# Folding the squares for the norm of an attention block, with the order of the step rewritten on three engines

## The chip, the cores and the metric

The kernel runs on one core of one Trainium2 chip. The metric is the device time of one execution in microseconds (us). The engines are named as in the profile: PE is TensorE (matmul), PEld its weight loads, DVE is VectorE, ACT is ScalarE, POOL is GpSimd, SP is SyncE, which issues most of the DMAs.

## What is computed

One block of a network with a gated, decaying linear attention in chunks of 128 positions, followed by a gated feed-forward layer. For a batch of 4 sequences of 256 positions, width 512, 32 heads of 128 in 8 groups that share keys and values:

```python
q = rope(h @ Wq.T); k = rope(h @ Wk.T); v = h @ Wv.T      # h: layernorm of x, modulated
decay = where(causal, exp(G_i - G_j), 0)                    # G: running sum of the decay rates in a chunk
y_intra = (q_i . k_j * decay) @ (v * dt)                    # inside a chunk
y_inter = (q * exp(G)) @ state                              # from the chunk before
y = y_intra + y_inter
rms = sqrt(mean(square(y), axis=-1) + 1e-5)                 # over the 128 of a head
y = y / rms * gnorm_w
y = y * (gate * sigmoid(gate))                              # gate = h @ Wg.T
x = x + ga * (y @ Wo.T)
x = x + gb * ffn(modulated layernorm of x)
```

The change lies in how `mean(square(y))` is summed over the 128 numbers of a head, and in the order in which the attention's work is issued.

## The kernel before

The attention loops over 8 groups of 4 heads (`groups`): seven passes of a hardware loop, and the last group written out. In a group there are 8 steps, `step(g, t)`, one for each tile of 128 positions; t // 2 is the sequence b, and c = t % 2 the chunk in it. "Even step" below is c = 0, "odd step" c = 1. The last four tiles of the last group have no projections left to do and are written as `tail`. The feed-forward layer follows and isn't touched.

The work on a tile is spread over two steps. Step t projects q and gate for four tiles ahead (`q_block`, `g_block`: 12 matmuls each, since every f32 product is made of three products of a rounded high part and a low part, lines L54 to L56), does the scores of tile t (`scores`, into ps_s) and its output (`y_product`, into ps_y), and multiplies the finished tile t - 1 by Wo (`out_product`, which needs z_hi and z_lo of tile t - 1). An even step also does the scores of the next chunk with this chunk's keys (`cross_scores`) and the keys and values of the next sequence (`kv_batch`, 24 matmuls of 256 columns); an odd step has a second product in `y_product` and transposes the keys (`k_turn`).

Each engine has its own queue and works through it in the order in which the code is written; there is no scheduler. Semaphores tie the queues together. The chain that turns ps_y into z runs over all of them: ACT squares ps_y, once in f32 into `work` and once rounded into `sq_hi`; DVE subtracts the two (`sq_lo`) and multiplies ps_y by the gate (into z); PE sums both parts over the 128 partitions with two matmuls by a matrix of ones (`square_sum`, L686 and L688, into ps_ss); ACT takes the logarithm (L854) and the exponential (L857) of it, `inverse_rms`; DVE multiplies z by that (`normed_z`); ACT rounds z to `z_hi` (L861), and DVE makes `z_lo`. Beside it ACT makes the gate's sigmoid in three passes, `exp_gate` (L755), and after DVE's `cap` (L980) a logarithm (L760) and an exponential (L762), `sigmoid`. `probabilities` (L1160) multiplies the scores by the decay on DVE. The squares, the probabilities and z share one buffer, `work`. POOL does one product of the rotation of each step (`rotate_q_sin`, L1299) and in even steps the causal mask of the next sequence (`mask`, L1292), which waits for `exp_g` on ACT (L770). Weights of the next group are split by DVE into high and low parts: one head in each of t = 1 to 4, keys and values at t = 5, and Wo at t = 0.

Of the kernel before, what the change touches and what calls it, by code (L numbers as in the profile page):

```python
# [10 lines left out]
P = 128  # L11
# [183 lines left out]
def block_attention(nc, cst, x1, hT_hi, hT_lo, tok, modT, gnorm, ident, modrow, gT_dram,  # L195
                    x_in, cT_in, wmod_in, wq_in, wg_in, wkv_in, wo_in, win_in, rows_in,
                    gnorm_in, cst_in, wgu_in, norm_rows, raw_pair):
    with ExitStack() as ctx:
        def sb(name, shape, dt=F32):
            return ctx.enter_context(nc.sbuf_tensor(name, shape, dt))  # L200
# [10 lines left out]
        wkv_hi, wkv_lo = (sb(n, [P, KT, 2 * D], F32R) for n in ("wkv_hi", "wkv_lo"))  # L211
        wo_hi, wo_lo = (sb(n, [P, GRP, HID], F32R) for n in ("wo_hi", "wo_lo"))
# [26 lines left out]
        prob_tail = sig[:].rearrange("p (h i) -> p h i", h=GRP)  # L239
# [10 lines left out]
        win, win_hi, win_lo = (w[:].rearrange("p (k h) -> p k h", k=KT) for w in (q_cos, sq_hi, sq_lo))  # L250
# [6 lines left out]
        zT = gT = [sq[0:H], rms[0:H]]  # L257
# [71 lines left out]
        sq_done = sem("sq_done")  # L329
        sqhi_done = sem("sqhi_done")  # L330
# [179 lines left out]
        def _(pe):  # L510
# [152 lines left out]
            def y_product(g, t, tail=False):  # L663
# [8 lines left out]
                weights = prob_tail if tail else prob[:]  # L672
                nc.tensor.matmul(ps_y[:], v[:, b % 2, c], weights.rearrange("p h i -> p (h i)"),  # L673
# [9 lines left out]
            def square_sum(g, t):  # L683

                pe.wait_ge(sqhi_done, g * 8 + (t + 1))
                nc.tensor.matmul(ps_ss[:], ones[:], sq_hi[:], start=True, stop=False)  # L686
                pe.wait_ge(sqlo_done, g * 8 + (t + 1))
                nc.tensor.matmul(ps_ss[:], ones[:], sq_lo[:], start=False, stop=True)\  # L688
                    .then_inc(ss_ready, 1)

            def step(g, t, project, next_batch, next_group):
# [4 lines left out]
                if project:  # L696
                    q_block(g, t)
                out_product(g, t)
                if c == 1 and next_batch:
                    k_turn(g, b)  # L700
                y_product(g, t)
                if project:
                    g_block(g, t, 0, KT - 1)
                square_sum(g, t)
                if project:
                    g_block(g, t, KT - 1, KT)
                if c == 0 and next_batch:
                    kv_batch(g, b)

            def tail(g, t):  # L710
# [5 lines left out]
                y_product(g, t, True)  # L716
# [27 lines left out]
        def _(act):  # L744
# [43 lines left out]

            def copy_kT(g, b):
# [54 lines left out]
            def squares(g, t, tail=False):  # L844
                if tail:
# [843 lines left out]
```

## Time and profile before

| | |
|---|---|
| median of 3 runs | 1111.58 us (1111.44 to 1113.81) |
| the profiled execution | 1113.59 us, its span 1111.8 us |
| PE busy | 1067.2 us, 96% |
| DVE busy | 767.0 us, 69% |
| ACT busy | 550.8 us, 50% |
| POOL busy | 206.1 us, 19% |
| mean granted clock of PE | 0.984 |

The span is the time from the first to the last instruction of the profiled execution. Busy times are sums of the durations of instructions; those of PE overlap, since a matmul starts before the one before it has ended, so starts tell more of PE than durations do. The granted clock is a share of 2.4 GHz.

### The profile page before, as it was taken

The page shows a single profiled execution, that of the slowest core. Times are in us where ns is not written, and L with a number is a line of the kernel's source. Part 1 is how long each engine was busy: PE and PEld are TensorE (multiplying, and loading weights), DVE is VectorE, ACT ScalarE, POOL GpSimd, SP SyncE. Part 2 cuts the span into 40 slices and gives each one's busy share as a digit, 9 for nine tenths or more (in the row PEclk, how much of TensorE's full clock was granted, in tenths as well). Part 3 has the DMA queues.
Part 4 walks back from the last instruction along what each step waited for, and adds up shares of the span by engine and source line. Part 5 has one row for each costly group of instructions (what it writes and reads, how often), then busy time and mean ns, then how long its engine had stood idle before and what let it go on. Part 6 is the DMA issues. An engine that isn't in the chain of part 4 may idle for free. (4 is left out here: it accounts for less than half of the span.)

```text
span 1111.8 us, 14213 instructions
## 1 busy us (share of the span) xinstructions
PE 1067.2 (96%) x4680; PEld 808.9 (73%) x4680; DVE 767.0 (69%) x1492; ACT 550.8 (50%) x1133; POOL 206.1 (19%) x131
## 2 busy tenths in 40 slices
PE   4879999999999999999999999999999969999898
PEld 1757777777777777777777777777776449888786
DVE  5777786877787678868876887778676686434411
ACT  3445556665555666555666555566655434222300
POOL 3412211212221121122111222211121530000000
PEclk9989999999999999999999999999999979999999
DMA  6121301220131013112201320131031622111011
GB/s 223 58 69 49 124 30 38 75 75 19 38 113 38 19 38 113 38 28 83 96 19 38 97 54 19 38 113 38 19 95 24 204 99 72 49 45 57 29 38 38
DMA packets 37464, 70.89 MB, mean 64 GB/s; under 512 B 2936, under 2 KB 19576, under 8 KB 35520
## 3 DMA queue, kind: packets, MB, share of 16 engines
q1 hardware_dynamic: 36720, 70.16, 19.9%
q10 hardware_dynamic: 720, 0.43, 0.1%
q8 instruction: 13, 0.21, 0.1%
q14 instruction: 11, 0.09, 0.0%
HBM read 68.33 MB, written 2.24 MB: 63 GB/s over the span
## 5 line engine op out<-in xcount | busy, mean ns | idle before, releaser
L1299 POOL TENSOR_TENSOR q_sin<-q_sin,cst 128x512 f32<-128x512 f32 x64 | 82.8, 1293 | 390.9 <-ACT q_sin L751 390.9
L1292 POOL TENSOR_TENSOR dec<-dec,future 128x1024 f32<-128x1024 f32 x31 | 80.3, 2590 | 273.6 <-ACT expg L770 273.6
L848 ACT ACTIVATE work<-ps_y 128x512 f32<-128x512 f32 x64 | 38.4, 599 | 186.4 <-PE ps_y L673 185.6
L54 PE MATMUL ps_gt<-hT_hi,wg_hi 128*128 128x512 f32 x256 | 125.7, 491 | 3.7 <-DVE sg L986 3.7
L54 PE MATMUL ps_q<-hT_hi,wq_hi 128*128 128x512 f32 x256 | 125.5, 490 | 2.8 <-DVE q_cos L966 2.3
L54 PE MATMUL ps_o<-wo_hi,z_hi 128*128 128x512 f32 x260 | 104.1, 400 | 2.4 <-DVE z_lo L49 2.4
L55 PE MATMUL ps_o<-wo_lo,z_hi 128*128 128x512 f32 x260 | 103.4, 398 | 0.0
L56 PE MATMUL ps_o<-wo_hi,z_lo 128*128 128x512 f32 x260 | 103.0, 396 | 0.0
L56 PE MATMUL ps_q<-hT_hi,wq_lo 128*128 128x512 f32 x256 | 101.2, 395 | 0.0
L55 PE MATMUL ps_gt<-hT_lo,wg_hi 128*128 128x512 f32 x256 | 100.7, 393 | 0.0
L56 PE MATMUL ps_gt<-hT_hi,wg_lo 128*128 128x512 f32 x256 | 100.7, 393 | 0.0
L55 PE MATMUL ps_q<-hT_lo,wq_hi 128*128 128x512 f32 x256 | 100.4, 392 | 0.0
L750 ACT ACTIVATE q_sin<-ps_q 64x512 f32<-64x512 f32 x64 | 38.1, 596 | 111.0 <-PE ps_q L56 110.9
L49 DVE TENSOR_TENSOR sq_lo<-work,sq_hi 128x512 fp32r<-128x512 f32 x64 | 44.6, 697 | 62.1 <-ACT sq_hi L849 62.1
L780 ACT ACTIVATE dec<-dec,scal 128x128 f32<-128x128 f32 x256 | 81.7, 403 | 1.4 <-DVE scal L944 1.4
L1160 DVE SCALAR_TENSOR_TENSOR work<-ps_s,scal,dec 128x128 f32<-128x128 f32 x240 | 67.6, 345 | 20.5 <-DVE z_lo L49 11.0
L1190 DVE TENSOR_TENSOR work<-work,rms 128x512 f32<-128x512 f32 x64 | 44.3, 692 | 52.4 <-ACT rms L857 52.4
L54 PE MATMUL ps_kv<-wkv_hi,hT_hi 128*128 128x256 f32 x256 | 73.6, 288 | 0.0
L55 PE MATMUL ps_kv<-wkv_lo,hT_hi 128*128 128x256 f32 x256 | 73.2, 286 | 0.0
L56 PE MATMUL ps_kv<-wkv_hi,hT_lo 128*128 128x256 f32 x256 | 73.1, 286 | 0.0
L966 DVE TENSOR_TENSOR q_cos<-ps_q,cst 128x512 f32<-128x512 f32 x64 | 44.1, 690 | 41.7 <-ACT q_sin L751 41.6
L54 PEld LDWEIGHTS ps_gt<-hT_hi,wg_hi 128*128 128x128 f32 x256 | 48.5, 189 | 27.0 <-issue 14.4
(239 smaller groups left out, 2553.0 us busy)
## 6 DMA issues: line engine op xcount, KB each, us to landing
dec<-gT_dram SPq DMA_DIRECT2D x32, 512.0 KB, 5.4
raw_q<-wq_in SPq DMA_DIRECT2D x32, 256.0 KB, 2.7
raw_g<-wg_in SPq DMA_DIRECT2D x32, 256.0 KB, 2.9
raw_o<-wo_in SPq DMA_DIRECT2D x8, 1024.0 KB, 7.3
raw_pair<-wkv_in SPq DMA_DIRECT2D x8, 512.0 KB, 4.7
raw_pair<-wgu_in SPq DMA_DIRECT2D x6, 512.0 KB, 3.3
raw_gu<-wgu_in SPq DMA_DIRECT2D x5, 512.0 KB, 3.4
qT<-wmod_in SPq DMA_DIRECT2D x2, 1024.0 KB, 7.0
```

Of the source, the lines that this page charges most:

```text
L49: return engine.tensor_tensor(lo, full, hi.bitcast(F32), ALU.subtract)
L54: pe.matmul(out, w_hi, x_hi, start=first, stop=False)
L55: pe.matmul(out, w_hi, x_lo, start=False, stop=False)
L56: return pe.matmul(out, w_lo, x_hi, start=False, stop=last)
L750: nc.scalar.activation(q_sin[0:64], ps_q[64:128, :], ACT.Copy)
L780: last = nc.scalar.activation(cell, cell, ACT.Exp, bias=scal[:, bn * CPB + c, 0, h:h + 1])
L848: nc.scalar.activation(sq, ps_y[:], ACT.Square).then_inc(sq_done, 1)
L966: nc.vector.tensor_tensor(q_cos[:].rearrange("p (b i) -> p b i", b=2), ps_q[:].rearrange("p (b i) -> p b i", b=2), cosT, ALU.mult)\
L1160: last = nc.vector.scalar_tensor_tensor(dest[:, h], ps_s[:, h * P:(h + 1) * P], scal[:, t, 1, h:h + 1], dec[:, b % 2, h, c], ALU.mult, ALU ...
L1190: nc.vector.tensor_tensor(z[:], z[:], rms[:].rearrange("p (h i) -> p h i", h=GRP), ALU.mult).then_inc(z_done, 1)
L1292: nc.gpsimd.tensor_tensor(cells, cells, future[:].unsqueeze(1).broadcast_to([P, GRP * CPB, CHUNK]), ALU.add).then_inc(mask_done, 1)
L1299: nc.gpsimd.tensor_tensor(q2, q2, sinT, ALU.mult).then_inc(qsin_done, 1)
```

## The change

The square of ps_y is now taken once, in two halves of 64 partitions (`sq_low`, `sq_top`); DVE adds the halves (`sum_squares`); ACT rounds the sum into the lower half of one tile, `sq_parts`, and DVE puts the low part into its upper half. One matmul by ones then sums high and low part together. `work` is replaced by three buffers of their own, and `win_lo` gets one of its own. The high parts of the weights are cast by ACT and no longer by DVE. And the order of the step is another on PE, ACT and DVE:

```diff
-        work = sb("work", [P, GRP, CHUNK])
-        prob, z = work, work
-        sq = work[:].rearrange("p h i -> p (h i)")
-        sq_hi, sq_lo = sb("sq_hi", [P, HALF], F32R), sb("sq_lo", [P, HALF], F32R)
+        prob, z = sb("prob", [P, GRP, CHUNK]), sb("z", [P, GRP, CHUNK])
+        sq_parts = sb("sq_parts", [P, HALF], F32R)
+        sq_top, sq_low = sb("sq_top", [P // 2, HALF]), sb("sq_low", [P // 2, HALF])
+        sq_sum = sb("sq_sum", [P // 2, HALF])
+        win_lo = sb("win_lo", [P, KT, P], F32R)
         rms = sb("rms", [P, HALF])
...
             def square_sum(g, t):
                 pe.wait_ge(sqhi_done, g * 8 + (t + 1))
-                nc.tensor.matmul(ps_ss[:], ones[:], sq_hi[:], start=True, stop=False)
                 pe.wait_ge(sqlo_done, g * 8 + (t + 1))
-                nc.tensor.matmul(ps_ss[:], ones[:], sq_lo[:], start=False, stop=True)\
+                nc.tensor.matmul(ps_ss[:], ones[:], sq_parts[:], start=True, stop=True)\
                     .then_inc(ss_ready, 1)
             def step(g, t, project, next_batch, next_group):
                     cross_scores(g, t)
                 if project:
                     q_block(g, t)
+                y_product(g, t)
                 out_product(g, t)
+                if project:
+                    g_block(g, t, 0, 2)
                 if c == 1 and next_batch:
                     k_turn(g, b)
-                y_product(g, t)
                 if project:
-                    g_block(g, t, 0, KT - 1)
-                square_sum(g, t)
-                if project:
-                    g_block(g, t, KT - 1, KT)
+                    g_block(g, t, 2, KT)
                 if c == 0 and next_batch:
                     kv_batch(g, b)
+                square_sum(g, t)
...
+            def round_squares(g, t):
+                act.wait_ge(sqsum_done, g * 8 + (t + 1))
+                nc.scalar.activation(sq_parts[0:64], sq_sum[:], ACT.Copy).then_inc(sqhi_done, 1)
...
-            def squares(g, t, tail=False):
-                if tail:
-                    act.wait_ge(zlo_done, g * 8 + (t + 1))
+            def squares(g, t):
                 act.wait_ge(y_ready, g * 8 + (t + 1))
-                nc.scalar.activation(sq, ps_y[:], ACT.Square).then_inc(sq_done, 1)
-                nc.scalar.activation(sq_hi[:], ps_y[:], ACT.Square).then_inc(sqhi_done, 1)
+                nc.scalar.activation(sq_low[:], ps_y[0:64], ACT.Square)
+                nc.scalar.activation(sq_top[:], ps_y[64:128], ACT.Square).then_inc(sq_done, 1)
+            def split_head_hi(g, j):
+                act.wait_ge(wh_loaded, g * 128 + 32 * (j + 1))
+                nc.scalar.activation(wq_hi[:, j], raw_q[:], ACT.Copy)
+                nc.scalar.activation(wg_hi[:, j], raw_g[:], ACT.Copy).then_inc(wh_hi_done, 1)
+            def split_kv_hi(g):
+                act.wait_ge(kv_loaded, g * 16 + 16)
+                nc.scalar.activation(wkv_hi[:], raw_kv[:], ACT.Copy).then_inc(kv_hi_done, 1)
+            def split_o_hi(g):
+                act.wait_ge(o_ready, g * 8 + 1)
+                act.wait_ge(wo_loaded, g * 16 + 16)
+                nc.scalar.activation(wo_hi[:], raw_o[:], ACT.Copy).then_inc(wo_hi_done, 1)
...
                 b, c = t // 2, t % 2
                 swap(g, t)
                 squares(g, t)
+                if next_group and 1 <= t <= GRP:
+                    split_head_hi(g + 1, t - 1)
+                if next_group and t == GRP + 1:
+                    split_kv_hi(g + 1)
+                round_squares(g, t)
                 if c == 1:
                     copy_kT(g, b)
                 decays(g, t + 1)
-                inverse_rms(g, t)
+                if t == 0:
+                    split_o_hi(g)
                 exp_gate(g, t)
-                split_z_hi(g, t)
-                sigmoid(g, t)
                 if c == 0:
+                    sigmoid(g, t)
+                    inverse_rms(g, t)
                     copy_v(g, b)
+                    split_z_hi(g, t)
                     exp_g(g, b)
+                else:
+                    inverse_rms(g, t)
+                    sigmoid(g, t)
+                    split_z_hi(g, t)
...
-            def probabilities(g, t, tail=False):
-                b, c = t // 2, t % 2
-                dest = prob_tail if tail else prob
-                if tail and t == 4:
-                    dve.wait_ge(sg_done, g * 8 + 8)
-                if not tail:
-                    dve.wait_ge(zlo_done, g * 8 + (t + 1))
+            def probabilities(g, t):
+                tile = t % NT
                 dve.wait_ge(s_ready, g * 8 + (t + 1))
                 dve.wait_ge(dec_done, g * 8 + (t + 1))
                 for h in range(GRP):
                     last = nc.vector.scalar_tensor_tensor(
-                        dest[:, h], ps_s[:, h * P:(h + 1) * P], scal[:, t, 1, h:h + 1],
-                        dec[:, b % 2, h, c], ALU.mult, ALU.mult)
+                        prob[:, h], ps_s[:, h * P:(h + 1) * P], scal[:, tile, 1, h:h + 1],
+                        dec[:, tile // 2 % 2, h, tile % 2], ALU.mult, ALU.mult)
                 last.then_inc(prob_done, 1)
+            def sum_squares(g, t):
+                dve.wait_ge(sq_done, g * 8 + (t + 1))
+                nc.vector.tensor_tensor(sq_sum[:], sq_low[:], sq_top[:], ALU.add).then_inc(sqsum_done, 1)
             def gated_y(g, t):
                 half = t // 4
-                dve.wait_ge(sqhi_done, g * 8 + (t + 1))
-                split_lo(nc.vector, sq_lo[:], sq, sq_hi[:]).then_inc(sqlo_done, 1)
-                dve.wait_ge(sqlo_done, g * 8 + (t + 1))
+                dve.wait_ge(zlo_done, g * 8 + (t + 1))
                 dve.wait_ge(sg_done, g * 8 + (4 * half + 4))
                 nc.vector.tensor_tensor(z[:], ps_y[:].rearrange("p (h i) -> p h i", h=GRP),
                                         sg[:, half, :, rows_of(t)], ALU.mult).then_inc(zz_done, 1)
+                dve.wait_ge(sqhi_done, g * 8 + (t + 1))
+                split_lo(nc.vector, sq_parts[64:128], sq_sum[:], sq_parts[0:64]).then_inc(sqlo_done, 1)
...
                 heads, keys = next_group and 1 <= t <= GRP, next_group and t == GRP + 1
-                probabilities(g, t)
+                gate(g, t - 1)
                 if c == 1:
                     rotate_k(g, b, t)
-                gate(g, t - 1)
                 rotate_q_cos(g, t)
                 if c == 0:
                     cross_probabilities(g, t)
-                if heads:
-                    split_head_hi(g + 1, t - 1)
-                if keys:
-                    split_kv_hi(g + 1)
+                sum_squares(g, t)
                 rotate_q_add(g, t)
+                gated_y(g, t)
                 add_out(g, t)
-                gated_y(g, t)
                 if heads:
                     split_head_lo_g(g + 1, t - 1)
+                    split_head_lo_q(g + 1, t - 1)
                 if keys:
                     split_kv_lo(g + 1)
                 if c == 0:
                     copy_scalars(g, b)
                 if t == 0:
-                    split_o_hi(g)
+                    split_o_lo(g)
+                probabilities(g, t + 1)
+                cap(g, t)
                 normed_z(g, t)
-                cap(g, t)
-                if heads:
-                    split_head_lo_q(g + 1, t - 1)
                 split_z_lo(g, t)
-                if t == 0:
-                    split_o_lo(g)
...
```

`tail` follows in the same manner: DVE's `sum_squares` stands ahead of `gated_y`, ACT's `round_squares` behind `squares`, `squares` no longer waits for z_lo, and the probabilities go to `prob` and not to the buffer of the sigmoid. Ahead of the loop DVE does the probabilities of tile 0.

ACT, an even step from the decays of the next tile to the rounding of expg (the names in brackets are the semaphores that a row waits for). Before:

```order
L780 ACTIVATE dec<-dec,scal 128x128 x4
L854 ACTIVATE rms<-ps_ss,eps_col 128x512 [waits ss_ready]
L857 ACTIVATE rms<-rms 128x512 [waits lnss_done]
L755 ACTIVATE sig<-ps_gt 128x512 [waits g_ready]
L861 ACTIVATE z_hi<-work 128x512 [waits z_done]
L760 ACTIVATE sig<-sig 128x512 [waits cap_done]
L762 ACTIVATE sig<-sig 128x512 [waits lsig_done]
L785 REGISTER_ALU
L787 ACTIVATE v<-ps_kv 128x256 [waits kv_ready]
L767 REGISTER_ALU
L770 ACTIVATE expg<-dec 128x512 [waits cross_done,dec_loaded]
```

The same stretch of an even step of the changed kernel:

```order
L790 ACTIVATE sq_parts<-sq_sum 64x512 [waits sqsum_done]
L779 ACTIVATE dec<-dec,scal 128x128 x4
L754 ACTIVATE sig<-ps_gt 128x512 [waits g_ready]
L759 ACTIVATE sig<-sig 128x512 [waits cap_done]
L761 ACTIVATE sig<-sig 128x512 [waits lsig_done]
L855 ACTIVATE rms<-ps_ss,eps_col 128x512 [waits ss_ready]
L858 ACTIVATE rms<-rms 128x512 [waits lnss_done]
L784 REGISTER_ALU
L786 ACTIVATE v<-ps_kv 128x256 [waits kv_ready]
L878 ACTIVATE z_hi<-z 128x512 [waits z_done]
L766 REGISTER_ALU
L769 ACTIVATE expg<-dec 128x512 [waits cross_done,dec_loaded]
```

The two passes of the sigmoid now stand ahead of the two of the inverse norm and of the rounding of z, where they stood behind all three.

DVE, from the end of an even step that splits a head (t = 4) into the odd one that follows. Before:

```order
L1190 TENSOR_TENSOR work<-work,rms 128x512 [waits rms_done,zz_done]
L980 TENSOR_SCALAR sig<-sig 128x512 [waits esig_done]
L49 TENSOR_TENSOR wq_lo<-raw_q,wq_hi 128x512
L49 TENSOR_TENSOR z_lo<-work,z_hi 128x512 [waits zhi_done]
L1160 SCALAR_TENSOR_TENSOR work<-ps_s,scal,dec 128x128 [waits dec_done,s_ready,zlo_done]
L1160 SCALAR_TENSOR_TENSOR work<-ps_s,scal,dec 128x128 x3
L950 REGISTER_ALU
L953 TENSOR_TENSOR q_cos<-ps_kv,cst 128x256 [waits rope_done,v_done]
L954 TENSOR_TENSOR q_cos<-ps_kv,cst 128x2x64
L956 TENSOR_TENSOR q_cos<-ps_kv,cst 128x2x64
L959 TENSOR_TENSOR kr<-q_cos 128x256 [waits kparts_done]
L986 SCALAR_TENSOR_TENSOR sg<-ps_gt,gnorm,sig 128x512 [waits sig_done]
```

The same place of the changed kernel:

```order
L1179 SCALAR_TENSOR_TENSOR prob<-ps_s,scal,dec 128x128 [waits dec_done,s_ready]
L1179 SCALAR_TENSOR_TENSOR prob<-ps_s,scal,dec 128x128 x3
L1004 TENSOR_SCALAR sig<-sig 128x512 [waits esig_done]
L1214 TENSOR_TENSOR z<-z,rms 128x512 [waits rms_done,zz_done]
L49 TENSOR_TENSOR z_lo<-z,z_hi 128x512 [waits zhi_done]
L1010 SCALAR_TENSOR_TENSOR sg<-ps_gt,gnorm,sig 128x512 [waits sig_done]
L974 REGISTER_ALU
L977 TENSOR_TENSOR q_cos<-ps_kv,cst 128x256 [waits rope_done,v_done]
L978 TENSOR_TENSOR q_cos<-ps_kv,cst 128x2x64
L980 TENSOR_TENSOR q_cos<-ps_kv,cst 128x2x64
L983 TENSOR_TENSOR kr<-q_cos 128x256 [waits kparts_done]
L989 REGISTER_ALU [waits kr_done]
```

The probabilities of the next tile, which wait for that tile's scores (s_ready), stood behind `cap`, `normed_z` and `z_lo`; now all three stand behind them.

## Rows read from the trace of the kernel before

**Rows 1.** The page: the span, and each engine's busy time, share and instructions.

```profile
span 1111.8 us, 14213 instructions
PE 1067.2 (96%) x4680; PEld 808.9 (73%) x4680; DVE 767.0 (69%) x1492; ACT 550.8 (50%) x1133; POOL 206.1 (19%) x131
```

**Rows 2.** Busy time by stretches: from:to, length, each engine's busy time, clock, DMA.

```profile
100.00:860.00 760.00, 760.00 (x3346) 574.87 (x3345) 578.32 (x1168) 445.60 (x916) 150.43 (x88) 1.00 0.19 56
```

**Rows 3.** Groups of instructions, 100 to 860: count | busy, mean ns | idle before.

```profile
L688 PE MATMUL ps_ss<-sq_lo,ones_r 128*128 128x512 f32 x59 | 23.3, 396 | 0.0
L750 ACT ACTIVATE q_sin<-ps_q 64x512 f32<-64x512 f32 x58 | 34.6, 596 | 103.9 <-PE ps_q L56 103.9
```

**Rows 4.** Timeline of PE, an even step and an odd one: start, us, instruction.

```profile
415.64 1.02 PE L659 MATMUL ps_s<-qT,kT 128*128 128x512 f32 x2
...
426.08 0.40 PE L688 MATMUL ps_ss<-sq_lo,ones_r 128*128 128x512 f32 x1
426.31 0.39 PE L54 MATMUL ps_gt<-hT_hi,wg_hi 128*128 128x512 f32 x1
...
429.87 1.02 PE L659 MATMUL ps_s<-qT,kT 128*128 128x512 f32 x2
...
433.48 0.40 PE L54 MATMUL ps_o<-wo_hi,z_hi 128*128 128x512 f32 x1
...
436.49 1.02 PE L668 MATMUL ps_y<-cross,v 128*128 128x512 f32 x2
437.36 1.02 PE L673 MATMUL ps_y<-work,v 128*128 128x512 f32 x2
...
441.45 1.02 PE L659 MATMUL ps_s<-qT,kT 128*128 128x512 f32 x2
```

**Rows 5.** Timeline of ACT over the same boundary between steps.

```profile
426.51 0.69 ACT L854 ACTIVATE rms<-ps_ss,eps_col 128x512 f32<-128x512 f32 x1 [0.29 <-PE ps_ss L688]
427.23 0.63 ACT L857 ACTIVATE rms<-rms 128x512 f32<-128x512 f32 x1
...
428.70 0.64 ACT L861 ACTIVATE z_hi<-work 128x512 fp32r<-128x512 f32 x1 [0.34 <-DVE work L1190]
429.23 0.62 ACT L760 ACTIVATE sig<-sig 128x512 f32<-128x512 f32 x1
429.88 0.63 ACT L762 ACTIVATE sig<-sig 128x512 f32<-128x512 f32 x1
430.42 0.36 ACT L787 ACTIVATE v<-ps_kv 128x256 f32<-128x256 f32 x1
```

**Rows 6.** Timeline of DVE over the same boundary.

```profile
427.97 0.69 DVE L1190 TENSOR_TENSOR work<-work,rms 128x512 f32<-128x512 f32 x1 [0.77 <-ACT rms L857]
428.58 0.42 DVE L980 TENSOR_SCALAR sig<-sig 128x512 f32<-128x512 f32 x1
...
429.51 0.69 DVE L49 TENSOR_TENSOR z_lo<-work,z_hi 128x512 fp32r<-128x512 f32 x1
430.99 1.13 DVE L1160 SCALAR_TENSOR_TENSOR work<-ps_s,scal,dec 128x128 f32<-128x128 f32 x4 [0.78 <-DVE z_lo L49]
...
432.88 1.18 DVE L959 TENSOR_TENSOR kr<-q_cos 128x256 f32<-128x256 f32 x1
...
435.52 1.01 DVE L44 CAST wq_hi<-raw_q 128x512 fp32r<-128x512 f32 x1
436.46 0.41 DVE L44 CAST wg_hi<-raw_g 128x512 fp32r<-128x512 f32 x1
```

**Rows 7.** Timeline of POOL in the odd step.

```profile
431.38 2.40 POOL L1292 TENSOR_TENSOR dec<-dec,future 128x1024 f32<-128x1024 f32 x1 [8.49 <-ACT expg L770]
434.96 1.29 POOL L1299 TENSOR_TENSOR q_sin<-q_sin,cst 128x512 f32<-128x512 f32 x1 [1.18 <-ACT q_sin L751]
```

**Rows 8.** Timeline of PE, two of its waits; the last is the tail's.

```profile
56.02 0.47 PE L54 MATMUL ps_q<-hT_hi,wq_hi 128*128 128x512 f32 x1 [2.27 <-DVE q_cos L966]
...
901.69 0.47 PE L54 MATMUL ps_o<-wo_hi,z_hi 128*128 128x512 f32 x1 [2.40 <-DVE z_lo L49]
```

**Rows 9.** PE by stretches behind those waits: length, busy, granted clock, DMA.

```profile
56.00:60.00 4.00, 2.96 (x12) 1.00 0.00 0
902.00:906.00 4.00, 4.00 (x12) 0.57 0.02 4
```

More of the change, by code:

```diff
@@ L210, in block_attention @@
         wg_hi, wg_lo = (sb(n, [P, GRP, KT, D], F32R) for n in ("wg_hi", "wg_lo"))
-        wkv_hi, wkv_lo = (sb(n, [P, KT, 2 * D], F32R) for n in ("wkv_hi", "wkv_lo"))
-        wo_hi, wo_lo = (sb(n, [P, GRP, HID], F32R) for n in ("wo_hi", "wo_lo"))
+        wo_hi, wo_lo = (sb(n, [P, GRP, HID], F32R, "right") for n in ("wo_hi", "wo_lo"))
+        wkv_hi, wkv_lo = (sb(n, [P, KT, 2 * D], F32R, "right") for n in ("wkv_hi", "wkv_lo"))
         raw_q, raw_g = sb("raw_q", [P, KT, D]), sb("raw_g", [P, KT, D])
@@ L249, in block_attention @@
         silu_c = sb("silu_c", [P, KT * B])
-        win, win_hi, win_lo = (w[:].rearrange("p (k h) -> p k h", k=KT) for w in (q_cos, sq_hi, sq_lo))
+        win, win_hi = (w[:].rearrange("p (k h) -> p k h", k=KT) for w in (q_cos, sq_parts))
         rows = cross[:, 1, 0:2 * H].rearrange("p (r h) -> p r h", r=2)
@@ L329, in block_attention @@
         sq_done = sem("sq_done")
+        sqsum_done = sem("sqsum_done")
         sqhi_done = sem("sqhi_done")
@@ L661, in scores, with y_product @@
                                  start=True, stop=True).then_inc(s_ready, 1)
-            def y_product(g, t, tail=False):
+            def y_product(g, t):
                 b, c = t // 2, t % 2
@@ L671, in y_product @@
                 pe.wait_ge(prob_done, g * 8 + (t + 1))
-                weights = prob_tail if tail else prob[:]
-                nc.tensor.matmul(ps_y[:], v[:, b % 2, c], weights.rearrange("p h i -> p (h i)"),
+                nc.tensor.matmul(ps_y[:], v[:, b % 2, c], prob[:].rearrange("p h i -> p (h i)"),
                                  start=c == 0, stop=True).then_inc(y_ready, 1)
@@ L715, in tail @@
                     out_product(g, t)
-                y_product(g, t, True)
+                y_product(g, t)
                 if c == 0:
@@ L881, in tail @@
                     decays(g, t + 1)
-                squares(g, t, True)
+                squares(g, t)
+                round_squares(g, t)
                 if t == 5:
@@ L1108, in _ @@
                     dve.wait_ge(win_split, 1)
-                    split_lo(nc.vector, win_lo, win, win_hi).then_inc(win_split, 1)
+                    split_lo(nc.vector, win_lo[:], win, win_hi).then_inc(win_split, 1)
             dve.wait_ge(tables_loaded, 16)
@@ L1234, in tail @@
                     gate(g, t - 1)
-                    probabilities(g, t, True)
                     add_out(g, t)
                     guard_gate(0)
+                sum_squares(g, t)
                 gated_y(g, t)
@@ L1243, in tail @@
                 if t < NT - 1 and t != 5:
-                    probabilities(g, t + 1, True)
+                    probabilities(g, t + 1)
                 if t == 4:
@@ L1254, in tail @@
                 if t == 5:
-                    probabilities(g, t + 1, True)
+                    probabilities(g, t + 1)
                 if t == 6:
@@ L1271, in stats_of @@
                 norm2.vector_stats(dve, tile)
+            probabilities(0, 0)
             groups(dve, step, tail)
```

10 lines of the change are left out of this document (3 added, 7 removed).

## The prediction

> **What bounds the kernel now.** I read the page first: PE is busy 96% of the span, DVE 69%, ACT 50% [rows 1]. A share is an average, so the next view is the stretch that holds the attention's loop, 100 to 860 us: PE is busy in all 760 of 760 us, DVE in 578, ACT in 446 [rows 2]. Busy times of PE overlap, so I checked starts on the timeline: matmuls of 512 columns start 0.23 us apart without a hole [rows 4], and the group of the second sum of squares has no idle time before it, 59 times out of 59 [rows 3]. In the loop nothing but the number of matmuls counts. Two steps take 441.45 - 415.64 = 25.81 us [rows 4].
>
> The other engines run in PE's shadow, and how much shadow there is can be read at the boundary from an even step to an odd one. The odd step's scores start at 429.87, the product by Wo at 433.48, 3.61 us later [rows 4]. It needs z_lo, which ends at 429.51 + 0.69 = 430.20 [rows 6], so 3.3 us early. The chain behind that is logarithm 426.51, exponential 427.23, z times it 427.97, z_hi 428.70, z_lo 429.51 [rows 5, 6]. It ends early because the sum of squares is done some 3.8 us ahead of the scores (426.08 against 429.87), and because ACT does the sigmoid's two passes behind z_hi [rows 5].
>
> **What goes.** One of the two matmuls by ones in each of the 64 tiles: 0.23 us from start to start [rows 4] (its busy 0.396 us [rows 3] is overlap). 0.46 us for a pair of steps, 14.7 us in all. This is the whole gain, as the loop has no other idle time of PE to win.
>
> **What moves, odd step.** The sum of squares now stands last in the step, the product of y ahead of the one by Wo, and on DVE the next tile's probabilities, which need the next scores, ahead of cap, z and z_lo. So z's chain can't end until the next step's scores have been done, and in even steps ACT puts the whole sigmoid ahead of the inverse norm. I lay the old durations along the new order, with 0 at the start of the odd step's scores. DVE starts the probabilities 430.99 - 429.87 = 1.12 after them and needs 1.13 [rows 4, 6]. DVE starts an independent instruction 0.08 before the last one ends (427.97 + 0.69 against 428.58), so cap runs from 2.17 to 2.59 [rows 6]. An engine takes up another's result 0.04 later (428.66 to 428.70): the sigmoid's logarithm starts at 2.63, its exponential 0.65 later at 3.28, the next independent pass 0.54 after that at 3.82, by the starts 429.23, 429.88, 430.42 [rows 5]. That pass is the logarithm of the squares; exponential 0.72 later at 4.54, until 5.17; z from 5.28 to 5.97 (0.11 and 0.69, as 427.86 to 427.97); z_hi from 6.01 to 6.65; z_lo from 6.69 to 7.38; PE can go on at 7.42 [rows 5, 6]. PE itself is there at 3.61, plus the two products of y that now come first, 0.87 each (436.49 to 437.36): 5.35 [rows 4]. **The product by Wo waits 2.07 us in every odd step.**
>
> **Even step.** There inverse_rms comes first, and only cap ties the chain to the scores: cap ends at 2.59, the sigmoid's passes start at 2.63 and 3.28, z_hi at 3.82, z_lo ends at 5.19, PE could go on at 5.23, and it arrives at 3.61 + 0.87 + 0.87 = 5.35 (cross scores and y) [rows 4 to 6]. It fits by 0.12 us. Where a head or the keys were split, DVE comes to the probabilities about 0.3 late, and PE waits 0.1 to 0.2. Over all pairs I take 0.1.
>
> **The sum of squares in odd steps.** z_lo is late, so are the mask, the keys and the squares behind it. ACT makes expg 0.54 after z_hi's start, at 6.55; it takes what the sigmoid's passes take, 0.62, and POOL's mask then runs 2.40, from 7.21 to 9.61 [rows 5, 7]. DVE comes to kr at about 8.8. Kr took 1.18 us and ended at 434.06, 0.28 after the mask's end at 433.78; the cast of wq_hi took 1.01 and ended at 436.53, 0.28 after POOL's product ended at 436.25, while the same cast beside an idle POOL took 0.41 [rows 6, 7]. So such a DVE instruction is held until POOL is through: kr ends at 9.9. POOL follows at once with its product (1.29, to about 11.0), and the new sum of the two halves, started at 10.4, is held until then and ends at 11.5. Rounding 11.6 to 12.2, and behind q's sum and the gated product the low part from 12.7 to 13.4. PE gets there at 7.42 + 24 x 0.23 + 0.22 for the transposes = 13.16. It waits 0.3 us more.
>
> The Trainium skill, "SBUF — State Buffer", section "Who interferes with whom", has the rule: a VectorE instruction with two SBUF inputs and a GpSimd instruction exclude each other, the later one blocked for the whole of the other. The two rows agree. With the rule the pair loses this 0.3 us, 9 us in all; if the new sum, on 64 partitions only, were not held, it would lose nothing here, and the total below would be 9 us lower.
>
> **Added work.** The squares are two passes on 64 partitions, where the nearest row is 0.596 us for 64x512 [rows 3], so they cost what the two old ones did. Rounding is one more such pass, the sum one more DVE instruction of 0.69; both are in the chain above. The weights' high parts on ACT: two casts a step, about 0.64 each, as z_hi [rows 5], keys and Wo two and four times that at most. They stand between the squares, done at about 9.0, and the rounding, which in odd steps waits for DVE until 11.5: hidden. If that cover were gone, they would cost at most 1.3 us in four steps of eight. The weights' loads wait for the low parts, which come earlier now, and those of the decays for the probabilities, also earlier: nothing on SP. The start of the loop costs nothing.
>
> **The tail.** Four tiles whose chain is exposed at the end (PE waits 2.40 for z_lo at 901.69 [rows 8]). Sum and rounding lengthen each tile's chain by 0.73 + 0.68, one square pass and one matmul go. Where other work of PE covers it, nothing is lost, and at all four 5 us. I take 2.
>
> **Sum.** The step runs 60 times, 30 pairs: -0.46 + 2.07 + 0.3 + 0.1 = +2.0 us, 60 us; with the tail 62. On the profiled span that is 1111.8 + 62 = 1174; this execution took 1113.59 us against a median of 1111.58 of the runs, so its span is as good a base as the median: 1174 us, 5.6% slower. (Of no change a measurement can tell about 0.2%.)
>
> **Rivals.**
> - The clock falls. PE sat still 2.40 us before 901.69, and in 902 to 906 the granted clock is 0.57, near the lower level of 1.2 GHz; after 2.27 us before 56.02 it stayed at 1.00 in 56 to 60 [rows 8, 9]. My 2.07 is below both, and PE is fully busy around it, which speaks against. If it fell each time as at 902, where (1 - 0.57) x 4 = 1.7 us of PE's work is lost, that would be 30 x 1.7 = 51 more, 1225; if at some, 1190 and up. 10%.
> - A shorter chain. If links are 0.1 faster in the new order, or the new sum isn't held by POOL, the odd step loses 1.3 to 2.0 instead of 2.4: 1140 to 1158. 9%.
> - More waits than I see (SP's loads, the keys, an even step that fits by 0.12 only): 0.5 us a pair and more, 1190 to 1205. 7%.
> - No slower at all: PE finds z_lo ready in the odd step. That needs the chain to end 5.31 us after the scores, not 7.38. It could if the inverse norm's 1.35 us ran while ACT waits for cap, which the queue's order forbids as a queue runs in its own order everywhere in this trace; then z would start at cap's end as in an even step, and only the saving would be left: 1111.6 - 13.8 + 2 = 1100. The deciding point is whether the logarithm of the squares starts before the scores are done. 4%.
>
> **How the numbers follow.** The forecast, 1158 to 1190, has 70%. For 8 in 10 I take in the upper part of the shorter chain and the lower part of more waits and the clock: 1152 to 1200. Slower 0.95, within 0.2% 0.01, faster 0.04, the last being the fourth rival's.
>
> **What the changed profile would show.** PE's idle before the first ps_o matmul (L54), released by z_lo, about 30 times and 50 to 65 us in all; the logarithm of ps_ss in even steps behind the sigmoid's exponential and 3.8 us after the scores' start; an idle before ps_ss of about 0.3 in odd steps, with the sum of squares longer than 0.69 beside POOL; pairs of 27.8 us instead of 25.8. A granted clock below 1.00 between 100 and 860 us would show the first rival; a z_lo that ends before the product of y the fourth.

## The result, and the profile after

The changed kernel takes 1202.51 us (median of 4 runs, 1199.5 to 1204.31) against 1112.69 of the kernel before beside it: ratio 1.079, 95% interval 1.076 to 1.081, 7.9% slower. The forecast, 1174 (range 1158 to 1190, 1152 to 1200 for eight in ten), had the sign and the place, and missed the size. The page of the changed kernel (span; busy time, share and instructions of each engine) answers to [rows 1]:

```profile
span 1201.6 us, 14252 instructions
PE 1089.0 (91%) x4616; PEld 805.2 (67%) x4616; DVE 775.1 (65%) x1485; ACT 651.5 (54%) x1268; POOL 205.2 (17%) x131
```

PE has 64 matmuls fewer and is busy only 91% of a longer span. The waits of the changed kernel from 100 to 930 us (engine, line and what it waited for: us in total, times, longest) say where it stands still:

```profile
PE ps_o L54 <- DVE z_lo L49: 56.7, 29, 2.0
PE ps_o L54 <- ACT z_hi L878: 1.9, 1, 1.9
PE ps_ss L687 <- DVE sq_parts L49: 1.8, 10, 0.2
```

So once in every odd step, 30 times, the product by Wo waits for z. How that comes about is on the timeline (start, duration, instruction, and in brackets the idle time before it) of one odd step and the start of the next, PE first:

```profile
439.11 1.02 PE L660 MATMUL ps_s<-qT,kT 128*128 128x512 f32 x2
...
443.57 1.02 PE L673 MATMUL ps_y<-prob,v 128*128 128x512 f32 x2
446.62 0.49 PE L54 MATMUL ps_o<-wo_hi,z_hi 128*128 128x512 f32 x1 [2.03 <-DVE z_lo L49]
446.95 0.39 PE L55 MATMUL ps_o<-wo_lo,z_hi 128*128 128x512 f32 x1
447.18 0.39 PE L56 MATMUL ps_o<-wo_hi,z_lo 128*128 128x512 f32 x1
...
452.27 0.40 PE L56 MATMUL ps_gt<-hT_hi,wg_lo 128*128 128x512 f32 x1
452.70 0.47 PE L687 MATMUL ps_ss<-sq_parts,ones_r 128*128 128x512 f32 x1
453.01 1.02 PE L660 MATMUL ps_s<-qT,kT 128*128 128x512 f32 x2
```

The same stretch on ACT and DVE:

```profile
441.66 0.63 ACT L759 ACTIVATE sig<-sig 128x512 f32<-128x512 f32 x1 [4.02 <-DVE sig L1004]
442.32 0.63 ACT L761 ACTIVATE sig<-sig 128x512 f32<-128x512 f32 x1
442.86 0.67 ACT L855 ACTIVATE rms<-ps_ss,eps_col 128x512 f32<-128x512 f32 x1
443.56 0.63 ACT L858 ACTIVATE rms<-rms 128x512 f32<-128x512 f32 x1
...
445.02 0.63 ACT L878 ACTIVATE z_hi<-z 128x512 fp32r<-128x512 f32 x1 [0.56 <-DVE z L1214]
```

```profile
440.17 1.13 DVE L1179 SCALAR_TENSOR_TENSOR prob<-ps_s,scal,dec 128x128 f32<-128x128 f32 x4 [0.83 <-PE ps_s L660]
441.21 0.42 DVE L1004 TENSOR_SCALAR sig<-sig 128x512 f32<-128x512 f32 x1
444.30 0.69 DVE L1214 TENSOR_TENSOR z<-z,rms 128x512 f32<-128x512 f32 x1 [2.67 <-ACT rms L858]
445.68 0.69 DVE L49 TENSOR_TENSOR z_lo<-z,z_hi 128x512 fp32r<-128x512 f32 x1 [0.69 <-ACT z_hi L878]
```

Read it as a chain from the scores: probabilities 1.06 after them, cap at 2.10, the sigmoid at 2.55, the logarithm of the squares only at 3.75, z_lo done at 7.26 (446.37). ACT sat still for 4.02 us before the sigmoid; in the last 2.4 of them, from 439.27 on, the squares' sum (the ps_ss matmul started at 438.88, for 0.39) lay ready. The forecast had 1.12, 2.17, 2.63, 3.82 and 7.38.

The second view is the granted clock (from:to, length, busy times, clock, DMA), over the loop and in the 3 us behind two such waits, after 1.93 us at 132.79 and after 1.93 us at 160.94:

```profile
100.00:930.00 830.00, 767.65 (x3256) 564.10 (x3255) 576.70 (x1147) 536.42 (x1035) 149.46 (x88) 0.98 0.17 51
132.99:135.99 3.00, 3.00 (x14) 2.44 (x14) 2.84 (x7) 2.89 (x6) 3.00 (x2) 1.00 0.00 0
161.14:164.14 3.00, 3.00 (x11) 2.36 (x11) 2.84 (x7) 2.79 (x5) 3.00 (x2) 0.71 0.00 0
```

In the second stretch 11 matmuls start instead of 14: for a part of it the clock was at its lower level, 1.2 GHz. This follows 11 of the 30 waits. An odd step without it takes 13.9 us (about 14.2 at t = 7), one with it 15.03 to 15.17.

The span cut at the loop's first scores and at the tail's:

| | before | changed | changed, second trace |
|---|---|---|---|
| start | 78.43 | 82.23 | 78.70 |
| loop, 60 steps | 775.96 | 854.87 | 854.57 |
| tail and feed-forward | 257.41 | 264.50 | 264.93 |
| span | 1111.8 | 1201.6 | 1198.2 |

### The profile page after: what moved, and what is told of

Read it like the earlier page. It is cut to its first block and busy times, and to the rows that moved or that the text cites. A ratio compares the mean times of both kernels' runs of the same rounds, so it can differ in the third digit from the quotient of the medians.

```text
span 1201.6 us, 14252 instructions
## 1 busy us (share of the span) xinstructions
PE 1089.0 (91%) x4616; PEld 805.2 (67%) x4616; DVE 775.1 (65%) x1485; ACT 651.5 (54%) x1268; POOL 205.2 (17%) x131
## 5 line engine op out<-in xcount | busy, mean ns | idle before, releaser
L54 PE MATMUL ps_o<-wo_hi,z_hi 128*128 128x512 f32 x260 | 115.3, 444 | 62.3 <-DVE z_lo L49 59.8
L759 ACT ACTIVATE sig<-sig 128x512 f32<-128x512 f32 x64 | 40.4, 632 | 182.2 <-DVE sig L1004 182.2
L1179 DVE SCALAR_TENSOR_TENSOR prob<-ps_s,scal,dec 128x128 f32<-128x128 f32 x256 | 72.0, 344 | 102.4 <-PE ps_s L660 102.4
L54 PEld LDWEIGHTS ps_o<-wo_hi,z_hi 128*128 128x128 f32 x260 | 52.3, 201 | 117.3 <-ACT z_hi L878 75.4
L56 PE MATMUL ps_o<-wo_hi,z_lo 128*128 128x512 f32 x260 | 110.5, 425 | 0.0
L54 PE MATMUL ps_gt<-hT_hi,wg_hi 128*128 128x512 f32 x256 | 105.2, 411 | 3.7 <-DVE sg L1010 3.7
L1214 DVE TENSOR_TENSOR z<-z,rms 128x512 f32<-128x512 f32 x64 | 44.1, 689 | 82.2 <-ACT rms L858 82.2
L49 DVE TENSOR_TENSOR z_lo<-z,z_hi 128x512 fp32r<-128x512 f32 x64 | 45.6, 712 | 60.3 <-ACT z_hi L878 60.3
L790 ACT ACTIVATE sq_parts<-sq_sum 64x512 fp32r<-64x512 f32 x64 | 40.5, 632 | 66.7 <-DVE sq_sum L1198 65.5
L660 PE MATMUL ps_s<-qT,kT 128*128 128x512 f32 x128 | 65.8, 596 | 3.8 <-DVE qT L998 3.2
```

The costliest lines, as they stand in the source:

```text
L49: return engine.tensor_tensor(lo, full, hi.bitcast(F32), ALU.subtract)
L54: pe.matmul(out, w_hi, x_hi, start=first, stop=False)
L56: return pe.matmul(out, w_lo, x_hi, start=False, stop=last)
L660: nc.tensor.matmul(ps_s[:].rearrange("p (h i) -> p h i", h=GRP), kT[:, b % 2, c * P:(c + 1) * P], qT[:, half, :, rows_of(t)], start=True, ...
L759: nc.scalar.activation(sig[:], sig[:], ACT.Ln, bias=1.0).then_inc(lsig_done, 1)
L790: nc.scalar.activation(sq_parts[0:64], sq_sum[:], ACT.Copy).then_inc(sqhi_done, 1)
```

## The experiments

The before runs beside the kernels have medians of 1113.2 to 1114.37 us. Fences below leave out what the text doesn't need.

**1 to 3: undo one move, the other, both.** ACT's (with c == 0):

```diff
                 if c == 0:
-                    sigmoid(g, t)
                     inverse_rms(g, t)
+                    sigmoid(g, t)
                     copy_v(g, b)
```

DVE's:

```diff
-                probabilities(g, t + 1)
                 cap(g, t)
+                probabilities(g, t + 1)
                 normed_z(g, t)
```

> Edit: in even steps ACT does the inverse norm ahead of the sigmoid again (as odd steps do); all else as in the changed kernel. Theory (the order on ACT makes z_lo late): the odd step's wait for z_lo before the product by Wo, 1.95 us in each of 30 odd steps, goes; z_lo then ends 5.2 us after the scores' start, PE comes at 5.35. With it the half-clock stretches behind these waits go (11 of them, 12.7 us of the loop). Left: waits before the sum of squares, 0.3 to 0.5 in odd steps. Time 1118 to 1132 us. Rival (the added work on ACT and DVE - casts, sum, rounding - is what PE waits for): z_lo stays late by a us or more, 1160 us or more.

> Edit: DVE does cap ahead of the next tile's probabilities; ACT's order as changed (sigmoid ahead of the inverse norm in even steps). Theory (cap waits for the next scores only because it is queued behind the probabilities): the sigmoid is then done before the next scores, the inverse norm starts on time, and nothing before the product by Wo waits. Time 1104 to 1114, about the kernel before or a little under it. Rival (ACT's order alone is the fault, as z waits for the inverse norm behind two more passes): the wait in odd steps shrinks to between 0.5 and 1.5 us, 1125 to 1160.

> Edit: both of these together. Theory: PE waits nowhere in the loop; only the saved matmul counts, 0.46 us a pair, 14 us, against some 7 us that the tail lost: 1103 to 1110, pairs of steps of 25.35 us. Rival (the added DVE and ACT work of the folded squares costs more than it saves): the sum of squares in odd steps waits 0.3 us or more, 1112 or more.

Measured: ACT's move undone 1133.16 us (ratio 1.0185, 1.0162 to 1.0209), DVE's undone 1109.64 (0.9964, 0.9953 to 0.9976), both undone 1102.71 (0.990, 0.9881 to 0.9918). The second lies in its interval; the first is 1.2 us above its own (1118 to 1132), the third 0.3 below (1103 to 1110). Odd steps take mostly 11.98, 11.33 and 11.33 us (12.3 in the first kernel at t = 7, 12.05 in the second at t = 1), even steps 14.21, 13.94 and 13.94: where DVE's move stays, even steps are 0.27 longer too. With both undone PE is without a hole again, as in [rows 2]; the window of the loop in that kernel:

```profile
100.00:830.00 730.00, 730.00 (x3241) 555.65 (x3240) 571.12 (x1138) 524.86 (x1024) 146.35 (x87) 1.00 0.19 58
```

and on ACT the logarithm doesn't wait for the sigmoid:

```profile
422.84 0.69 ACT L855 ACTIVATE rms<-ps_ss,eps_col 128x512 f32<-128x512 f32 x1 [2.50 <-PE ps_ss L687]
423.56 0.64 ACT L858 ACTIVATE rms<-rms 128x512 f32<-128x512 f32 x1
424.10 0.61 ACT L759 ACTIVATE sig<-sig 128x512 f32<-128x512 f32 x1
```

What follows: the long wait before the product by Wo is the work of the two moves together. Against both undone, ACT's order alone costs 7 us, DVE's alone 30, both 100 us: either engine's order alone still leaves a way on which the squares' norm doesn't go through the next scores; together they close it. With DVE's move alone z still stands behind the probabilities, and z_lo ends 5.36 us after the scores, 0.03 too late for PE: its start behind that and a wait before the sum of squares make the odd step 0.65 longer.

**4 and 5: fill the wait.** Into the changed kernel, between v's product and Wo's in odd steps, 8 matmuls whose result nobody reads (1.84 us), or 3 (0.69 us):

```diff
                 y_product(g, t)
+                if c == 1:
+                    for _ in range(8):      # 3 in the other kernel
+                        nc.tensor.matmul(ps_x[:], ones[:], hT_hi[:, 0, 0:HALF], start=True, stop=True)
                 out_product(g, t)
```

> Edit: the changed kernel, with 8 matmuls of 512 columns by ones into ps_x, which nobody reads then, put into the gap of the odd step between the product of y and the product by Wo (8 x 0.23 = 1.84 us in a gap of about 2.1). No wait is taken away. Theory (the idle gap makes the granted clock fall in about one odd step of three, which costs 12.7 us of the loop): no stretch at half clock in the loop, odd steps all 13.7 to 13.9 us, 1187 to 1192 us. Rival (the clock falls for another reason, or the long steps have another cause): still 15.06 us in a third of the odd steps, and 1202 us or more.

> The changed kernel with three products whose result nobody reads between v's product and Wo's in the odd steps (0.69 us of the about 2 us that TensorE waits there). Eight of them kept the clock at 1.00 through the loop and took 11 us off the span. Theory (the clock falls because of the length of the uninterrupted idle stretch, which is 1.3 us now): no half-clock stretch in the loop, every odd step 13.9 us, 1190 to 1193 us as with eight. Rival (it is the amount of work in the step, which three products change little): odd steps of 15.0 us remain, 4 to 11 of them, 1195 to 1202 us.

Measured: 1191.55 us (1.071, 1.0684 to 1.0737) and 1192.33 (1.071, 1.0687 to 1.0734), some 10 us under the changed kernel with more work for PE. The waits and the clock with three:

```profile
PE ps_o L54 <- DVE z_lo L49: 36.6, 29, 1.3
```

```profile
100.00:920.00 820.00, 776.65 (x3345) 568.93 (x3344) 576.12 (x1150) 535.62 (x1033) 150.71 (x88) 1.00 0.17 52
```

The 30 waits are 1.20 to 1.34 us long, and the clock is at 1.00 throughout; both times lie in their intervals; all odd steps but t = 7 take 13.9 us, those about 14.2. The loop takes 844.54 us instead of 854.57 to 854.87: the clock's part of the loss is 10.2 us. (An odd step with the half clock loses 1.15 us, but the even step behind it is 0.3 shorter, 13.95 against 14.24, presumably since the other engines have caught up.) So the falls come from the idle time before the product by Wo. Whether the length of the one wait decides, as I expected, or the idle time of the whole step, is not shown: three products shorten both at once, and no run parts them.

**6 and 7: a longer wait, and the changed kernel again.** One more pass on ACT in even steps, behind the sigmoid; nobody reads what it writes:

```diff
                     sigmoid(g, t)
+                    nc.scalar.activation(sq_low[:], sq_top[:], ACT.Copy)
                     inverse_rms(g, t)
```

> The changed kernel with one more pass of ScalarE on 64 partitions, whose result nobody reads, between the sigmoid and the logarithm of the squares in the even steps. TensorE's wait for z_lo in the odd steps is then longer by about 0.53 us, 2.5 instead of 1.9 to 2.0. In the changed kernel 11 of the 30 waits of 1.89 to 2.03 us were followed by a stretch at half clock; of the waits of 2.27 to 2.61 us at the start and the end of ten traces 16 of 19 were. Theory (how often the clock falls goes with the length of the wait): 20 or more of the 30 waits are followed by a stretch at half clock, so 30 x 0.53 = 16 us for the wait and 9 to 19 more stretches of 1.15 us, 10 to 22 us: 1225 to 1242 us. Rival (which waits it falls after is set by something else, such as the place in the program): again about 11, so 16 us more than the changed kernel, 1216 to 1221.

> The changed kernel once more, for a second trace of it. Theory (the fall of the clock after a wait of 1.9 to 2.0 us is a matter of chance): another set of 6 to 16 odd steps has the stretch at half clock, the other odd steps take 13.9 us, and the start of the loop, 3.8 us late in the first trace, is at 78 to 82 us. Rival (it belongs to certain steps): the same 11 steps. The time is 1198 to 1205 us by either.

Measured: 1221.66 us (1.0984, 1.0947 to 1.1021) and 1200.54 (1.0789, 1.0755 to 1.0822). The waits are now 2.40 to 2.57 us, and 17 of 30 are followed by a lower clock, two of them here:

```profile
130.34:133.34 3.00, 3.00 (x14) 2.42 (x14) 2.84 (x7) 2.89 (x6) 3.00 (x2) 1.00 0.00 0
159.05:162.05 3.00, 3.00 (x9) 2.32 (x9) 2.84 (x7) 2.80 (x5) 3.00 (x2) 0.58 0.00 0
```

More than 11, fewer than the 20 I expected; 30 x 0.51 = 15.3 us of wait and six more such stretches make up the loop's 21 us (875.69 against 854.7). The time, 1221.66, lies between the two intervals, 1216 to 1221 and 1225 to 1242. The theory holds in direction, my size of it doesn't. The second trace of the changed kernel has again 11 falls of 30, but in other steps: only four waits of the thirty are hit in both. They are spread evenly, behind every second to fourth wait and never behind two in a row; with the longer waits two in a row occur three times. What picks them stays open. The time, 1200.54, lies in the interval that both shared, 1198 to 1205. The start is at 78.70, so the 3.8 us at the start of the first trace weren't the change's.

**8: the tail without the fold.** On top of both moves undone, the last four tiles alone square 128 partitions twice and sum with two matmuls:

```diff
+                nc.scalar.activation(sig[:], ps_y[:], ACT.Square)
+                nc.scalar.activation(sq_parts[:], ps_y[:], ACT.Square).then_inc(sqhi_done, 1)
...
+                pe.wait_ge(sqhi_done, g * 8 + (t + 1))
+                nc.tensor.matmul(ps_ss[:], ones[:], sq_parts[:], start=True, stop=False)
+                pe.wait_ge(sqlo_done, g * 8 + (t + 1))
+                nc.tensor.matmul(ps_ss[:], ones[:], win_lo[:].rearrange("p k h -> p (k h)"),
+                                 start=False, stop=True).then_inc(ss_ready, 1)
```

> The kernel with both moves undone in ScalarE's and VectorE's order (rms ahead of the sigmoid, cap ahead of the next probabilities), and in the last four tiles alone the squares are not folded: two squares of 128 partitions, one subtraction, two products by ones. In the folded version of that kernel the tail has waits for sq_parts of 0.48, 1.74, 2.26 and 0.95 us, 5.4 in all, where the kernel before has 0.34. Theory (the fold's longer chain square, sum, rounding, rest is the whole loss of the tail): the waits go but for about 0.3, four products of 0.23 come back, so the tail is about 258 instead of 263.2 us and the time about 1098 us (1096 to 1100). Rival (the tail loses by the order of its other work, not by the fold): the tail stays above 261.5 and the time at 1101 to 1104.

Measured: 1098.08 us (0.986, 0.984 to 0.9881), the best kernel of the study; its tail takes 256.97 us. The time lies in its interval, the tail 1 us under the 258 expected. The timeline of PE in the tail of the kernel with the fold (both moves undone), where the sum waits in all four tiles:

```profile
851.74 0.47 PE L687 MATMUL ps_ss<-sq_parts,ones_r 128*128 128x512 f32 x1 [0.48 <-DVE sq_parts L49]
...
861.96 0.47 PE L687 MATMUL ps_ss<-sq_parts,ones_r 128*128 128x512 f32 x1 [1.74 <-DVE sq_parts L49]
...
874.64 0.58 PE L687 MATMUL ps_ss<-sq_parts,ones_r 128*128 128x512 f32 x1 [2.26 <-DVE sq_parts L49]
...
885.65 0.47 PE L687 MATMUL ps_ss<-sq_parts,ones_r 128*128 128x512 f32 x1 [0.95 <-DVE sq_parts L49]
```

Ahead of the wait at 861.96, ACT and DVE in that kernel show what the fold's chain is there:

```profile
858.00 0.59 ACT L850 ACTIVATE sq_top<-ps_y 64x512 f32<-64x512 f32 x1
858.63 1.51 DVE L1198 TENSOR_TENSOR sq_sum<-sq_low,sq_top 64x512 f32<-64x512 f32 x1 [0.16 <-ACT sq_top L850]
...
860.17 0.63 ACT L790 ACTIVATE sq_parts<-sq_sum 64x512 fp32r<-64x512 f32 x1 [1.58 <-DVE sq_sum L1198]
860.84 0.98 DVE L49 TENSOR_TENSOR sq_parts<-sq_sum,sq_parts 64x512 fp32r<-64x512 f32 x1
```

Three links, sum, rounding, rest, where there was one (the rest), and the sum takes 1.51 us beside POOL's additions (four from 856.59 on) instead of 0.67. That the waits are the fold's is shown, since without it 0.6 us of the 5.4 are left (0.32 and 0.28, in two of the tiles).

**9: no fold at all in the good order.** Two squares of 128 partitions, one subtraction and two matmuls by ones in every step:

```diff
-                nc.scalar.activation(sq_low[:], ps_y[0:64], ACT.Square)
-                nc.scalar.activation(sq_top[:], ps_y[64:128], ACT.Square).then_inc(sq_done, 1)
+                nc.scalar.activation(sq_full[:], ps_y[:], ACT.Square)
+                nc.scalar.activation(sq_parts[:], ps_y[:], ACT.Square).then_inc(sqhi_done, 1)
...
-                nc.tensor.matmul(ps_ss[:], ones[:], sq_parts[:], start=True, stop=True)\
+                nc.tensor.matmul(ps_ss[:], ones[:], sq_parts[:], start=True, stop=False)
+                nc.tensor.matmul(ps_ss[:], ones[:], win_lo[:].rearrange("p k h -> p (k h)"),
+                                 start=False, stop=True)\
```

> The same kernel with both moves undone and the fold taken out everywhere (two squares of 128 partitions, one subtraction, two products by ones in every step); the step's order and ScalarE's weight casts stay. Theory (TensorE is never late in that loop, so the one product less is all that the fold gives): every step is longer by 0.23, 11.56 and 14.17 us, the loop by about 60 x 0.23 = 14 us, the tail shorter by about 5, so about 1111 us (1109 to 1114), the time of the kernel before. Rival (the reordered step gives something of its own): 1108 or less, even steps under 14.1. Rival (the longer list of waits of the fold costs more than the product): 1105 or less, steps not longer.

Measured: 1114.55 us (1.0005, 0.9991 to 1.002), the time of the kernel before. It is half a microsecond above the expected 1109 to 1114. Steps of 11.59 and 14.19 us against 11.33 and 13.94 with the fold: 0.26 and 0.25, the price of one matmul (0.23) and a little. What is left of the reordered step, without the two moves, gives nothing by itself.

**10: the casts on DVE again**, Wo's at t = 0 too, both moves undone:

```diff
                 if c == 0:
                     cross_probabilities(g, t)
+                if heads:
+                    split_head_hi(g + 1, t - 1)
+                if keys:
+                    split_kv_hi(g + 1)
                 sum_squares(g, t)
```

> The same kernel with both moves undone, the high parts of the weights cast by VectorE again, in front of the sum of the squares. Theory (the folded step has filled VectorE and the cast's place is in front of the chain to the product by ones, so ScalarE's casts are needed): the odd steps with a cast (t = 1 and 3) and t = 5 are longer by 0.2 to 0.7 us and show a wait for sq_parts, 1.2 us per group, so 1108 to 1112 us. Rival (the casts lie beside TensorE's work on either engine): steps of 11.33 and 13.94 as without the move, 1102 to 1104 us.

Measured: 1108.55 us (0.9954, 0.9936 to 0.9972). The time lies in my interval, the mechanism only in part: t = 1 and 3 take 11.52 instead of 11.33 and t = 5 11.46, 0.5 us a group instead of 1.2, and no wait for sq_parts over 0.25 us shows in the loop. In seven groups that is 3.5 us. The loop is only 2.0 longer than with the casts on ACT, since its first step took 14.04 us here and 15.68 there (clock 0.89 in it); the rest of the 4.5 us between the two spans is the tail, 1.9, and the start, 0.65. So the casts' move is worth some 3.5 us in the loop. In the tail the sum's second wait is 2.82 us here against 1.74, with a lower clock behind it; in the changed kernel the same wait was 1.74 us in one execution and 2.81 in the other, so the casts need not be the reason of the tail's 1.9.

## Why the prediction was right on the place and short on the size

The steps that failed are three terms of the sum: the wait's cost beside its length, with the even steps (10.5 us more than forecast), the granted clock, a rival at 10% that the sum priced at nothing (10.2 us), and the tail (5.3 us). So two of the rivals came true together, "the clock falls" and, with 0.35 us a pair instead of 0.5, "more waits than I see". No single one of the three would have led out of the range.

*Right: the matmul saved.* -0.46 a pair; experiment 9 measures 0.51.

*Right: the product by Wo waits in every odd step, by both moves together.* Each link of the chain in the step shown came within 0.12 us up to z_lo's end, and experiments 1 to 3 show that the two moves make the wait. The last rival, no slower at all, needed the logarithm ahead of the scores; it starts 3.75 us after them.

*Short by 10.5 us: what a wait costs beside its length.* I took up a result 0.04 us after its end, as ACT and DVE do [rows 5, 6]. PE takes longer: 446.62 - 446.37 = 0.25 us after z_lo's end in the step shown, as at each t = 1, and 0.15 us in most other odd steps, as here at t = 3 (474.55 to 474.70):

```profile
473.86 0.69 DVE L49 TENSOR_TENSOR z_lo<-z,z_hi 128x512 fp32r<-128x512 f32 x1 [0.69 <-ACT z_hi L878]
474.70 0.47 PE L54 MATMUL ps_o<-wo_hi,z_hi 128*128 128x512 f32 x1 [1.93 <-DVE z_lo L49]
475.00 0.40 PE L55 MATMUL ps_o<-wo_lo,z_hi 128*128 128x512 f32 x1
```

The next matmul comes 0.30 to 0.34 later instead of 0.23. The odd step lost 2.32 us (13.90 against 11.58), where 2.07 + 0.30 - 0.23 = 2.14 was forecast, and at t = 7 some 0.3 more, between the sum of squares and the next scores (0.58 instead of 0.31); its cause stays open. The even step, which "fits by 0.12 us", doesn't fit: in the kernel with three matmuls it takes 14.20 on the mean, not 14.10. In the changed kernel's step from 453.01 DVE begins the probabilities 1.38 us after the scores instead of 1.12, z_lo ends 5.41 after them instead of 5.19, and PE starts 0.15 behind that. Experiments 1 to 3 show it to be DVE's move: without it the even steps take 13.94. In the kernel with three matmuls, free of the clock, a pair takes 13.95 + 14.20 = 28.15 us, 2.35 more than before, not 2.0; 30 x 0.35 = 10.5. Its loop, 844.54 us, is nevertheless only 68.6 longer than the 775.96 of before, since the first step of before took 15.94 us, of which the half clock was the reason (behind a wait of 2.57 us at 78.43), and that one 14.06: 1.9 back. The window of before over it:

```profile
78.00:86.00 8.00, 7.57 (x22) 5.10 (x23) 2.49 (x7) 3.37 (x8) 0.00 (x0) 0.79 0.72 214
```

[Rows 8] had the sign of the restart: a matmul of 0.47 behind the wait, where others show 0.40.

*Wrong: "My 2.07 is below both", 10% for the clock.* I had two waits, one of 2.27 us without a fall and one of 2.40 with one [rows 8, 9], and read an order into them. In the traces of before, of the changed kernel and of eight others (all but experiments 6 and 7) the same two places show waits of 2.27 to 2.61 us, 19 in all, as the one at the start is shorter, 1.76 us, in the changed kernel. 16 of the 19 were followed by a lower clock in the 4 us behind them; the quiet one in the trace of before was one of three exceptions. At 1.89 to 2.03 us it is 11 of 30, twice, at 1.20 to 1.34 none of 30. At 2.40 to 2.57 in experiment 6 it is 17 of 30. At this one place of the loop the share grows with the length of the wait, with no sharp edge. But the place counts as well: the wait for the loop's first scores was followed by a lower clock in 4 of the 12 traces only, though it lasts 2.50 to 3.23 us, and the longest of these, in the changed kernel, had none behind it (the wait in brackets, and the clock, 1.00, in a window behind it):

```profile
82.23 1.13 PE L660 MATMUL ps_s<-qT,kT 128*128 128x512 f32 x2 [3.23 <-DVE qT L998]
82.43:85.43 3.00, 3.00 (x11) 1.79 (x11) 1.86 (x6) 1.67 (x4) 0.00 (x0) 1.00 0.92 319
```

So 16 of 19 holds for two places and isn't a rate for waits of that length. The price, 1.7 us a fall, was too high; 11 of them cost 10 us.

*Short by 5.3 us: the tail.* I took 2 of the 5 us at most, for "where other work of PE covers it, nothing is lost". It covered little: the tail lost 7.1 and 7.5 us, 6.2 of it the fold's (263.20 against 256.97 in experiments 3 and 8). The bound was low too, since it took DVE's sum at 0.69, not 1.51.

*Right: the sum of squares in odd steps,* 0.3 forecast: in the step shown ps_ss starts 0.43 after the matmul before it instead of 0.23, and the scores 0.31 after that, 0.28 in all. At t = 3 it is 0.56 and 0.31, 0.41 in all, which is a part of the 10.5 above. DVE's sum beside POOL, and the same instruction in the next step, where POOL was done in time, in the changed kernel:

```profile
449.66 0.97 DVE L1198 TENSOR_TENSOR sq_sum<-sq_low,sq_top 64x512 f32<-64x512 f32 x1
...
460.63 0.67 DVE L1198 TENSOR_TENSOR sq_sum<-sq_low,sq_top 64x512 f32<-64x512 f32 x1
```

```profile
448.61 1.48 POOL L1318 TENSOR_TENSOR q_sin<-q_sin,cst 128x512 f32<-128x512 f32 x1
```

It ends 0.54 us after POOL does (450.63 against 450.09). By the rule of the Trainium skill, "SBUF — State Buffer", section "Who interferes with whom", an instruction of VectorE with two inputs in SBUF and one of GpSimd that reads SBUF keep each other out; the trace agrees for 64 partitions too. Of the two rows that the prediction took as agreeing with this rule only kr's is such an instruction; the cast of wq_hi has one input, and shows the delay (1.01 us instead of 0.41) without being a case of the rule as the prediction tells it. The exclusion itself was not switched off in any run. The prediction also gave it two prices: its sum makes the total 9 us lower without it, 1165, its rival 1140 to 1158.

*The account.* 62 us forecast, 10.5 for the restarts and the even steps, 1.9 back at the first step, 10.2 for the clock, 5.3 for the tail: 86.1, on 1111.8 gives 1197.9 us; the second trace has a span of 1198.2, the first 3.4 more by its start.

## What to carry to other kernels

Of an engine's order ask which instructions lie on a chain that crosses a boundary between steps, and whether one of them now stands behind something that needs the next step's first result: two reorderings that cost 7 and 30 us alone cost 100 together, because each blocked the other's way round. Two waits, one with a fall of the clock and one without, are no threshold; count all waits of about that length, at every place and in all traces at hand, before ruling a rival out. And a longer chain that hides in a full loop comes to light in the tail, where the old form can stay: here that was worth another 4.6 us of 1102.7.

## What the hardware showed that I had not expected

- The granted clock fell to its lower level behind 11 of 30 nearly equal waits of 1.89 to 2.03 us, in two executions, in different steps.
- The same clock stayed at 1.00 behind a wait of 3.23 us at another place of the same execution (82.23 us).
- PE starts 0.15 to 0.25 us after the end of the DVE instruction that it waits for, and 0.07 to 0.11 us more goes before its second matmul, where ACT and DVE take up a result after some 0.04 us.
- The time that the start of the kernel takes varies by 3.5 us between two executions of the changed kernel (first scores of the loop at 78.70 and 82.23 us); in the other ten traces they stand at 78.10 to 80.35.
